# Third layer normalisation moved into the expert loop of a transformer-mixer kernel, near experts' gating and summing fused, output stored by batch

## The chip, the cores and the metric

The kernel runs on one core of a Trainium2 chip. The time is device microseconds of one execution; a measured time is the median of several runs. The core's engines are TensorE (PE, with PEld for its weight loads), VectorE (DVE), ScalarE (ACT), GpSimd (POOL) and SyncE (SP), which here only issues DMA. Everything is float32.

## What is computed

The input x has 8 batches of 512 tokens, 128 features each. Four residual steps follow, each on a layer-normalised x:

```python
x = x + attention(layernorm(x))       # 16 heads, top-k, relative positions: most of the time
x = x + ffn(layernorm(x))             # experts, first call
x = x + mixer(layernorm(x))           # a state-space mixer; step sizes softplus(xn @ W_dt + bias)
x = x + ffn(layernorm(x))             # experts, second call, same weights
```

`ffn` has 8 experts. Each token goes to the expert with the largest logit, if fewer than 512 tokens before it went there; its output is gate * (xn @ W_e + b_e). The kernel computes all eight experts' products for each token and multiplies them by eight gates, of which at most one is not zero, then adds the eight results and the bias product gates @ b.

## The kernel before

**Layout.** The stream `k.X` is [128, 4096] in SBUF: 32 tiles of 128 tokens (partitions) by 128 features. A group is four tiles, 512 tokens, one batch; there are 8 groups. `k.XNT` is the normalised stream, transposed, features on the partitions. Both stay in SBUF for the whole kernel. There are eight PSUM banks of 128 x 512.

**Order of the program.** `attention`, `experts` (first call), `norm`, `mixer`, `norm`, `experts` (second call), `store_stream`. Each part is one or more blocks; a block has one instruction stream per engine, the engines meet only in semaphores, and all engines end a block together. Attention already contains the second normalisation by groups (`group_stats`, `group_rstd`, `group_scale`, `group_turn`, `group_keep`, `group_products`), so the first call of `experts` begins with finished logits in bank 3.

**The helpers by group**, all of which exist before the change and are used in attention: `group_stats` (VectorE, L204: four bn_stats, four bn_aggr, one addition; raises `vareps`), `group_rstd` (GpSimd, L217: a power; raises `rstd`), `group_scale` (VectorE, L223: four tensor_scalar of 128 x 128, (x - mean) * rstd with two scalars from SBUF, L227; raises `scaled`), `group_turn` (TensorE, L232: waits for `scaled`, four transposes into one bank; raises `turned`), `group_keep` (ScalarE, L242: bank to XNT; raises `kept`), `group_products` (TensorE, L248: waits for `kept`, four 128 x 8 products, which the trace shows as eight instructions).

**`norm`** (L1934) normalises all 32 tiles in a block of its own: statistics, powers, scaling, transposes, copies. After it the mixer makes all step sizes in one go (`eight_tensor`, L1223: 32 products of eight columns, 64 instructions) into bank 0, and VectorE copies them (L1233).

**`experts`**, its first block: softmax, place in the expert's queue and the gates `b.gate8` [128, 256], a chain mostly on VectorE. Its second block is the expert loop, written with `two_at_a_time` (two rounds written out, then a hardware loop over pairs, addresses from registers). For each group i:

- SP copies the group's 512 columns of XNT to `xs` and its gates to `gs` by DMA inside SBUF.
- TensorE transposes the gates of the four tiles to bank 4 or 5, then for each tile c makes two products of 512 columns: near (experts 0 to 3) into bank 0 or 2, far (experts 4 to 7) into bank 1 or 3. Each is two instructions in the trace. Behind tile 0 it makes the bias products of the whole group into bank 6 or 7. It waits for `near_scaled` and `far_scaled` of the tile two before, which used the same banks.
- ScalarE copies the turned gates (`gt`), then scales the far bank, four passes of 128 columns each with one gate column (L1401), into `far`.
- VectorE multiplies the near bank with the gates in one pass of 512 columns into `near` (L1426), adds `far` into `sums` (L1418), and adds the bias bank to the stream once a group (L1435).
- GpSimd adds the eight parts of each token: 1024 columns (L1448), 512 (L1451), then into the stream (L1456). It starts when all four tiles of a group are summed (`summed`) and raises `stream_added`.

**`store_stream`** writes all of X to DRAM in one DMA behind the last block.

Of the kernel before, what the change touches and what calls it, by code (L numbers as in the profile page):

```python
# [16 lines left out]
P = 128  # L17
# [1222 lines left out]
def experts(nc, sem, sb, ps, k, r, tag, made=None):  # L1240
# [5 lines left out]
    xs_in = [S(f"xs_in{q}") for q in range(2)]  # L1246
    gs_in = [S(f"gs_in{q}") for q in range(2)]
    g_turned, g_kept, bias_made, bias_added = (S(n) for n in ("g_turned", "g_kept", "bias_made", "bias_added"))

    near_made, y_made, near_scaled, far_scaled = (S(n) for n in ("near_made", "y_made", "near_scaled", "far_scaled"))  # L1250
# [19 lines left out]
    xs = [sb(f"{tag}_xs{q}", [P, 512]) for q in range(2)]  # L1270
    gs = [sb(f"{tag}_gs{q}", [P, 4 * E]) for q in range(2)]
    gt = [sb(f"{tag}_gt{q}", [E, 512]) for q in range(2)]
    near = [sb(f"{tag}_near{q}", [P, 512]) for q in range(2)]
# [67 lines left out]

    with nc.Block() as block:
        @block.sync
        def _(sp):
            def body(i, par, first):
                at, gates_at, free, turned = known(sp, i * 512, i * 4 * E, (i - 1) * 4, i - 1)
                if not first:
                    sp.wait_ge(y_made, free)
                sp.dma_start(xs[par][:, :], k.XNT[:, bass.ds(at, 512)]).then_inc(xs_in[par], 16)  # L1349
                if not first:  # L1350
                    sp.wait_ge(g_turned, turned)
                sp.dma_start(gs[par][:, :], b.gate8[:, bass.ds(gates_at, 4 * E)]).then_inc(gs_in[par], 16)

            two_at_a_time(sp, GROUPS, body)

        @block.tensor
        def _(pe):
            def body(i, par, first, half=0):
                pe.wait_ge(gs_in[par], (half + 1) * 16)
                if not first:  # L1360
                    pe.wait_ge(g_kept, i - 1)
                for c in range(4):
                    last = nc.tensor.transpose(ps[4 + par][0:E, c * P:(c + 1) * P], gs[par][:, c * E:(c + 1) * E],  # L1363
                                               k.ident[:, :])
                last.then_inc(g_turned, 1)
                pe.wait_ge(xs_in[par], (half + 1) * 16)
                for c in range(4):
                    for q in range(2):
                        bank = ps[2 * (c % 2) + q]
                        if not (first and par == 0 and c < 2):  # L1370
# [4 lines left out]
                            .then_inc((near_made, y_made)[q], 1)  # L1375
                    if c == 0:

                        pe.wait_ge(g_kept, i + 1)
                        if not first:
                            pe.wait_ge(bias_added, i - 1)  # L1380
                        for cc in range(4):
                            last = nc.tensor.matmul(ps[6 + par][:, cc * P:(cc + 1) * P],  # L1382
                                                    gt[par][:, cc * P:(cc + 1) * P], r.eb[:, :], start=True, stop=True)
                        last.then_inc(bias_made, 1)

            two_at_a_time(pe, GROUPS, body, with_half=True)

        @block.scalar
        def _(act):
            def body(i, par, first):  # L1390
                act.wait_ge(g_turned, i + 1)
                if not first:
                    act.wait_ge(bias_made, i - 1)
                nc.scalar.activation(gt[par][:, :], ps[4 + par][0:E, :], ACT.Copy).then_inc(g_kept, 1)

                for c in range(4):
                    act.wait_ge(y_made, i * 4 + c + 1)
                    if not (first and par == 0 and c < 2):
                        act.wait_ge(summed, i * 4 + c - 1)
                    for e in range(4):  # L1400
                        last = nc.scalar.activation(far[c % 2][:, e * P:(e + 1) * P],  # L1401
                                                    ps[2 * (c % 2) + 1][:, e * P:(e + 1) * P],
                                                    ACT.Copy, scale=b.gate8[:, bass.ds((i * 4 + c) * E + 4 + e, 1)])
                    last.then_inc(far_scaled, 1)

            two_at_a_time(act, GROUPS, body)

        @block.vector
        def _(dve):
            def body(i, par, first):  # L1410
                def add(c):

                    t = i * 4 + c
                    dve.wait_ge(near_scaled, t + 1)
                    dve.wait_ge(far_scaled, t + 1)
                    if c == 0 and not first:
                        dve.wait_ge(stream_added, i - 1)
                    nc.vector.tensor_tensor(sums[par][:, c, :], near[c % 2][:, :], far[c % 2][:, :],  # L1418
                                            ALU.add).then_inc(summed, 1)

                for c in range(4):
                    t = i * 4 + c
                    dve.wait_ge(near_made, t + 1)
                    if not (first and par == 0 and c < 2):
                        dve.wait_ge(summed, t - 1)
# [4 lines left out]
                    if c > 0:  # L1430
                        add(c - 1)
                    else:
                        X4 = k.X[:, bass.ds(i * 512, 512)]
                        dve.wait_ge(bias_made, i + 1)
                        nc.vector.tensor_tensor(X4, ps[6 + par][:, :], X4, ALU.add).then_inc(bias_added, 1)  # L1435
                add(3)

            two_at_a_time(dve, GROUPS, body)

        @block.gpsimd  # L1440
        def _(pool):

            def body(i, par, first):
                four = sums[par][:, :, :].rearrange("p t (e f) -> p t e f", e=4)
                pool.wait_ge(summed, i * 4 + 4)
                if not early(i):
# [8 lines left out]
                X4 = k.X[:, bass.ds(i * 512, 512)].rearrange("p (t f) -> p t f", t=4)  # L1455
                nc.gpsimd.tensor_tensor(X4, one_sum[:, :, :], X4, ALU.add).then_inc(stream_added, 1)  # L1456

            two_at_a_time(pool, GROUPS, body)
# [6 lines left out]
def mixer(nc, sem, sb, ps, k, r):  # L1465
# [3 lines left out]
    g = eight_sems(sem, "mixer_dt")  # L1469
# [14 lines left out]
    with nc.Block() as block:  # L1484
        @block.tensor
        def _(pe):
            eight_tensor(nc, pe, g, r.wdt[:, :], k.XNT, ps[0])

# [17 lines left out]
        def _(dve):  # L1506
            eight_vector(nc, dve, g, b.raw, ps[0])
            dve.wait_ge(g.stored, 1)
# [450 lines left out]
def store_stream(nc, sem, k, out):  # L1959
    done = sem("stream_stored")  # L1960
    with nc.Block() as block:
        @block.sync
        def _(sp):
            sp.dma_start(out.rearrange("b (t p) d -> p (b t) d", p=P),
                         k.X[:, :].rearrange("p (t d) -> p t d", d=D)).then_inc(done, 16)
# [101 lines left out]
```

## Time and profile before

| | us |
|---|---|
| median of 3 runs | 2992.06 (2991.2 to 2996.38) |
| the profiled execution's own time | 2988.63 |
| its span, first to last instruction | 2986.9 |
| attention and everything before it, until the first logits | 2359.9 |
| first expert loop, first transposes to last sums | 73.1 |
| from there to the mixer's copy of the step sizes | 41.9 |
| second expert loop | 72.3 |
| from the last sums to the end of the span | 14.7 |

How the views are read: a row of the windows view has start and end of a stretch, its length, the busy us and number of instructions of PE, PEld, DVE, ACT and POOL, then PEclk (TensorE's granted clock, 1.00 is full speed), the share of the DMA engines and GB/s. A row of the timeline has start, length, engine, line, operation, the tensors written and read, their sizes, how many instructions of that kind follow each other (x4: the length is that of all four) and in brackets how long the engine was idle before and which instruction released it. Lengths of neighbours on one engine overlap a little, since the next one starts while the last one drains. A row of groups has busy us and mean ns of one.

### The profile page before, as it was taken

The numbers are of one execution on the slowest core, as the hardware profiler recorded it, in microseconds if no ns is written. First come the engines' busy times: TensorE is split into PE (matmuls) and PEld (weight loads), VectorE is DVE, ScalarE is ACT, GpSimd is POOL, SyncE is SP. The second block draws the span as 40 slices with busy tenths as digits, with TensorE's granted clock in tenths as the row PEclk, the third lists the DMA queues.
The fourth block names the chain that finished last, engine by engine and source line by source line (L and its number), as shares of the span: only waits on it lengthen the run. The fifth ranks groups of instructions, "written<-read, shape, count | busy, mean of one in ns | idle before, by whom it ended". The sixth has DMA issues, their size and how long they took to land. (4 is left out here: it accounts for less than half of the span.)

```text
span 2986.9 us, 56920 instructions
## 1 busy us (share of the span) xinstructions
PE 2534.7 (85%) x16480; PEld 1489.4 (50%) x16480; DVE 2680.1 (90%) x6614; ACT 2062.6 (69%) x6275; POOL 2254.1 (75%) x2816
## 2 busy tenths in 40 slices
PE   5788888888888888888888888888888777988857
PEld 3444444444444444444544444444444436777743
DVE  7999999999999999999999999999999374776546
ACT  3788888888888788888887878888887342222214
POOL 4899999998998999999999989999998251222105
PEclk8899999999999999999999999999999786776659
DMA  4444444444444444444444444444443000000001
GB/s 123 121 120 118 121 121 120 121 121 120 120 121 115 120 119 124 121 123 119 122 117 118 123 117 120 122 120 124 119 121 101 12 19 15 8 8 0 1 12 47
DMA packets 373454, 286.18 MB, mean 96 GB/s; under 512 B 30174, under 2 KB 369192, under 8 KB 373160
## 3 DMA queue, kind: packets, MB, share of 16 engines
q1 hardware_dynamic: 372232, 280.62, 33.0%
q8 instruction: 129, 2.11, 0.3%
q10 hardware_dynamic: 928, 2.10, 0.2%
q14 instruction: 165, 1.35, 0.1%
HBM read 139.48 MB, written 136.58 MB: 92 GB/s over the span
## 5 line engine op out<-in xcount | busy, mean ns | idle before, releaser
L1038 DVE MAX8 top<-work 128x8 f32<-128x512 f32 x1536 | 982.8, 684 | 0.0
L1047 DVE MATCH_REPLACE8 work<-top,work 128x512 f32<-128x512 f32 x1024 | 687.4, 682 | 0.0
L1124 POOL TENSOR_TENSOR scores<-scores,cut 128x512 f32<-128x512 f32 x512 | 642.0, 1276 | 0.0
L657 PE MATMUL bank<-probs_t,u 128*64 128x512 f32 x2048 | 476.8, 608 | 10.9 <-ACT u L893 1.4
L1116 POOL TENSOR_SCALAR cut<-scores,minus_max_and_least 128x512 f32<-128x512 f32 x512 | 354.2, 692 | 46.9
L945 ACT ACTIVATE probs_of_tile<-scores,minus_max_and_least 128x512 f32<-128x512 f32 x512 | 376.2, 767 | 14.4 <-POOL scores L1124 14.4
L1137 POOL TENSOR_SCALAR probs_of_tile<-probs_of_tile,inverse 128x512 f32<-128x512 f32 x512 | 349.2, 692 | 26.9 <-DVE inverse L1004 1.4
L1047 DVE MATCH_REPLACE8 work<-top,scores 128x512 f32<-128x512 f32 x512 | 343.6, 682 | 0.0
L1035 DVE MAX8 top<-scores 128x8 f32<-128x512 f32 x512 | 326.7, 683 | 5.2 <-ACT scores L886 4.9
L1120 POOL TENSOR_SCALAR cut<-cut 128x512 f32<-128x512 f32 x512 | 305.6, 613 | 21.5
L864 ACT ACTIVATE band<-band 128x129 f32<-128x129 f32 x512 | 155.2, 304 | 225.1 <-DMA band<-probs_scratch 224.2
L886 ACT ACTIVATE scores<-bank 128x512 f32<-128x512 f32 x512 | 273.3, 584 | 45.1 <-PE bank L706 45.0
L910 ACT ACTIVATE probs_t<-bank 128x512 f32<-128x512 f32 x512 | 282.0, 609 | 11.4 <-PE bank L753 10.3
L753 PE MATMUL bank<-identity,probs_of_tile 128*128 128x128 f32 x2048 | 278.4, 281 | 4.1 <-POOL probs_of_tile L1137 4.1
L657 PEld LDWEIGHTS bank<-probs_t,u 128*64 128x64 f32 x2048 | 137.8, 139 | 267.8 <-issue 228.0
L741 PE MATMUL bank<-identity,band 128*128 128x128 f32 x512 | 109.8, 297 | 185.5 <-ACT band L873 184.1
L657 PE MATMUL bank<-probs_t,v 128*64 128x384 f32 (+1 forms) x2048 | 255.4, 392 | 0.0
L753 PEld LDWEIGHTS bank<-identity,probs_of_tile 128*128 128x128 f32 x2048 | 242.7, 145 | 4.5 <-POOL probs_of_tile L1137 4.5
L657 PEld LDWEIGHTS bank<-probs_t,v 128*64 128x64 f32 x2048 | 124.3, 139 | 173.1 <-ACT probs_t L910 99.0
L1769 POOL TENSOR_TENSOR mixer_a_spread<-rest_after,mixer_a 128x1024 f32<-128x1024 f32 x32 | 66.4, 2075 | 168.8 <-PE bank L1626 137.6
L678 PE MATMUL bank<-keys_left,qt 64*128 64x64 f32 (+3 forms) x1024 | 185.5, 439 | 1.3 <-ACT scores L886 1.3
L923 ACT ACTIVATE rel<-bank 128x254 f32<-128x254 f32 x512 | 174.3, 414 | 1.9 <-PE bank L694 1.9
(274 smaller groups left out, 5005.6 us busy)
## 6 DMA issues: line engine op xcount, KB each, us to landing
probs_scratch<-probs_of_tile SPq DMA_DIRECT2D x256, 256.0 KB, 2.4
band<-probs_scratch SPq DMA_DIRECT2D x256, 256.0 KB, 3.2
rel_scratch<-rel SPq DMA_DIRECT2D x256, 254.0 KB, 3.1
relj<-rel_scratch SPq DMA_DIRECT2D x256, 128.0 KB, 2.3
relj<-rel_scratch SPq DMA_DIRECT2D x512, 64.0 KB, 2.4
experts_xs<-stream_normed_t SPq DMA_DIRECT2D x16, 256.0 KB, 2.3
stream<-in_L_attn_a_x SPq DMA_DIRECT2D x4, 512.0 KB, 7.9
mixer_xs<-stream_normed_t SPq DMA_DIRECT2D x8, 256.0 KB, 2.4
```

The lines of the kernel that those rows point to most:

```text
L657: last = nc.tensor.matmul(U[HEADS[h], lo:hi], lhs, pt[mpar][:, h, jt, lo:hi], start=(jt == 0 and lo == 0), stop=(jt == NT - 1 and step > 0))
L753: last = nc.tensor.transpose(PT[h][:, jt * P:(jt + 1) * P], t.prob[Td][:, h, HALF + jt * P:HALF + (jt + 1) * P], k.ident[:, :])
L886: nc.scalar.activation(sc[Tb][:, h, :], SC[h][:, :], ACT.Copy).then_inc(s.scores_kept, 1)
L910: nc.scalar.activation(pt[dpar][:, h, :, Td * P:(Td + 1) * P], PT[h][:, :].rearrange("p (j i) -> p j i", j=NT), ACT.Copy).then_inc(s.probs ...
L945: nc.scalar.activation(t.prob[Tx][:, h, HALF:HALF + N], sc[Tx][:, h, :], ACT.Exp, bias=neg[q][:, h, 0:1], accum_out=rs[Tx][:, h:h + 1]).th ...
L1035: nc.vector.max(top[q][:, h, 0:8], sc[Tc][:, h, :]).then_inc(s.tops, 1)
L1038: nc.vector.max(top[q][:, h, 8 * rnd:8 * rnd + 8], work[:, h, :]).then_inc(s.next_tops, 1)
L1047: nc.vector.match_replace(out=work[:, h, :], in_to_replace=top[q][:, h, 8 * rnd:8 * rnd + 8], in_values=sc[Tc][:, h, :] if rnd == 0 else w ...
L1116: nc.gpsimd.tensor_scalar(cut[:, h, :], sc[Tc][:, h, :], neg[q][:, h, 1:2], STEEP, ALU.add, ALU.mult).then_inc(s.compared, 1)
L1120: nc.gpsimd.tensor_scalar(cut[:, h, :], cut[:, h, :], 0.0, NEG, ALU.min, ALU.max).then_inc(s.cut, 1)
L1124: nc.gpsimd.tensor_tensor(sc[Tc][:, h, :], sc[Tc][:, h, :], cut[:, h, :], ALU.add).then_inc(s.masked, 1)
L1137: nc.gpsimd.tensor_scalar(row, row, inv[Ty][:, h:h + 1], 1.0, ALU.mult, ALU.mult).then_inc(s.probs, 1)
```

## The change

1. The expert loops are written out, all eight groups, with constant addresses. The copies to `xs` and `gs` go away: TensorE reads XNT and `gate8` directly. Gates use bank 4 alone, bias products bank 6 alone.
2. Near experts: the multiplication into `near` and the addition into `sums` become four scalar_tensor_tensor passes of 128 columns, near bank * gate + far. They wait for `near_made` and `far_scaled`; TensorE waits for `summed` instead of `near_scaled`.
3. The first call of `experts` gets `follow`, the semaphores of a third normalisation by groups, made with the helpers above inside the loop. The step sizes' products go to bank 7. The `norm` block ahead of the mixer and the mixer's own `eight_tensor` go away.
4. The second call gets `out`: SP stores each group when it is finished. `store_stream` goes away.

```diff
+    GT, TURN, BIAS, EIGHT = ps[4:8]
+        if out is not None:
+            @block.sync
+            def _(sp):
+                for i in range(GROUPS):
+                    sp.wait_ge(stream_added, i + 1)
+                    sp.dma_start(out[i, :, :].rearrange("(t p) d -> p t d", p=P),
+                                 k.X[:, i * 512:(i + 1) * 512].rearrange("p (t d) -> p t d", d=D)).then_inc(out_stored, 16)
...
         @block.tensor
+            def late(i):
+                group_turn(nc, pe, follow, i, gw.xn[:, i % 2, :], TURN, k.ident, 1)
+            for i in range(GROUPS):
...
+                    last = nc.tensor.transpose(GT[0:E, c * P:(c + 1) * P], b.gate8[:, at:at + E], k.ident[:, :])
                 last.then_inc(g_turned, 1)
+                if follow and i >= 2:
+                    late(i - 2)
                 for c in range(4):
                     for q in range(2):
-                            pe.wait_ge((near_scaled, far_scaled)[q], i * 4 + c - 1)
-                        nc.tensor.matmul(bank[:, :], xs[par][:, c * P:(c + 1) * P],
+                        if t >= 2:
+                            pe.wait_ge((summed, far_scaled)[q], t - 1)
+                        nc.tensor.matmul(ps[2 * (c % 2) + q][:, :], k.XNT[:, t * P:(t + 1) * P],
...
+                    if c == 2 and follow and i >= 2:
+                        group_products(nc, pe, follow, i - 2, follow.W, k.XNT, EIGHT)
+            if follow:
+                for i in range(GROUPS - 2, GROUPS):
+                    late(i)
+                    group_products(nc, pe, follow, i, follow.W, k.XNT, EIGHT)
...
         @block.scalar
+                    if c == 0 and follow and i >= 2:
+                        group_keep(nc, act, follow, i - 2, TURN, k.XNT)
...
         @block.vector
+            def stats(i):
+                dve.wait_ge(stream_added, i + 1)
+                group_stats(nc, dve, follow, gw, k.X, i)
+            def scale(i):
+                if i >= 2:
+                    dve.wait_ge(follow.turned, i - 1)
+                group_scale(nc, dve, follow, gw, k.X, i, gw.xn[:, i % 2, :])
+            for i in range(GROUPS):
                 for c in range(4):
                     t = i * 4 + c
                     dve.wait_ge(near_made, t + 1)
-                    nc.vector.tensor_tensor(near[c % 2][:, :].rearrange("p (e f) -> p e f", e=4),
-                                            ps[2 * (c % 2)][:, :].rearrange("p (e f) -> p e f", e=4),
-                                            b.gate8[:, bass.ds(t * E, 4)].unsqueeze(2).to_broadcast([P, 4, P]),
-                                            ALU.mult).then_inc(near_scaled, 1)
+                    dve.wait_ge(far_scaled, t + 1)
+                    for e in range(4):
+                        cols = slice(e * P, (e + 1) * P)
+                        last = nc.vector.scalar_tensor_tensor(
+                            out=sums[par][:, c, cols], in0=ps[2 * (c % 2)][:, cols],
+                            scalar=b.gate8[:, t * E + e:t * E + e + 1], in1=far[c % 2][:, cols],
+                            op0=ALU.mult, op1=ALU.add)
+                    last.then_inc(summed, 1)
...
+                    if c == 2 and follow and i:
+                        stats(i - 1)
+                if follow and i:
+                    scale(i - 1)
+            if follow:
+                stats(GROUPS - 1)
+                scale(GROUPS - 1)
...
         @block.gpsimd
                 nc.gpsimd.tensor_tensor(X4, one_sum[:, :, :], X4, ALU.add).then_inc(stream_added, 1)
+                if follow:
+                    group_rstd(nc, pool, follow, gw, i)
...
 in mixer:
-            eight_tensor(nc, pe, g, r.wdt[:, :], k.XNT, ps[0])
-            eight_vector(nc, dve, g, b.raw, ps[0])
+            dve.wait_ge(made.products, GROUPS)
+            nc.vector.tensor_copy(b.raw[:, :], ps[7][:, 0:n8]).then_inc(raw_kept, 1)
...
 in program:
+            experts(nc, sem, allocate(ctx), ps, k, r, "experts1", norm2, norm3, gw)
+            mixer(nc, sem, allocate(ctx), ps, k, r, norm3)
         norm(nc, norms, ps, k, w)
+            experts(nc, sem, allocate(ctx), ps, k, r, "experts2", out=out)
```

## Rows read from the trace of the kernel before

**Rows 1.** Windows by stage (columns are explained above): first loop, behind it, the mixer.
```profile
2372.59:2445.67 73.08, 71.00 (x224) 34.10 (x224) 53.21 (x72) 40.17 (x136) 35.28 (x21) 0.97 0.08 27
...
2445.67:2487.57 41.90, 22.12 (x96) 19.44 (x96) 17.98 (x81) 4.78 (x8) 10.83 (x5) 0.54 0.00 0
...
2487.57:2850.89 363.32, 308.12 (x1574) 251.30 (x1574) 228.47 (x641) 98.74 (x191) 74.78 (x40) 0.69 0.02 6
```

**Rows 2.** Timeline of the second expert loop, TensorE and ScalarE.
```profile
2910.31 1.88 PE L1373 MATMUL bank<-rest_we,experts_xs 128*128 128x512 f32 x4
...
2913.21 5.42 PE L1373 MATMUL bank<-rest_we,experts_xs 128*128 128x512 f32 x12
...
2915.23 1.14 ACT L1401 ACTIVATE experts_far<-bank,experts_gate 128x128 f32<-128x128 f32 x4 [1.86 <-PE bank L1373]
...
2916.95 1.14 ACT L1401 ACTIVATE experts_far<-bank,experts_gate 128x128 f32<-128x128 f32 x4 [0.57 <-PE bank L1373]
...
2961.83 1.88 PE L1373 MATMUL bank<-rest_we,experts_xs 128*128 128x512 f32 x4
```

**Rows 3.** Chain that ended last: start us, us, what; handover from ScalarE to VectorE.
```profile
2919.43 0.39 ACT experts_far L1401
...
2919.91 0.70 DVE experts_sums L1418
```

**Rows 4.** Groups of VectorE by line and shape, whole span.
```profile
L1426 DVE TENSOR_TENSOR experts_near<-bank,experts_gate 128x512 f32<-128x512 f32 x64 | 44.2, 690 | 24.7 <-PE bank L1373 19.2 <-DVE experts_sums L1418 5.1
...
L1805 DVE SCALAR_TENSOR_TENSOR mixer_sum_x<-mixer_conv_x,rest_cwx,mixer_sum_x 128x512 f32<-128x512 f32 x24 | 17.7, 737 | 0.0
...
L1877 DVE TENSOR_TENSOR stream<-bank,stream 128x128 f32<-128x128 f32 x16 | 4.6, 286 | 15.5 <-PE bank L1676 15.5
```

**Rows 5.** Timeline at the end of set_up: scaling alone, then beside GpSimd.
```profile
34.46 1.11 DVE L227 TENSOR_SCALAR probs_t<-stream,group_mean_var,group_rstd 128x128 f32<-128x128 f32 x4
...
38.05 2.49 POOL L1068 TENSOR_TENSOR stream<-stream,attention_out_bias 128x512 f32<-128x512 f32 x2
...
38.11 2.52 DVE L227 TENSOR_SCALAR probs_t<-stream,group_mean_var,group_rstd 128x128 f32<-128x128 f32 x2
```

**Rows 6.** Timeline of the last 15 us.
```profile
2971.54 0.69 DVE L1418 TENSOR_TENSOR experts_sums<-experts_near,experts_far 128x512 f32<-128x512 f32 x1 [0.40 <-ACT experts_far L1401]
...
2972.31 2.34 POOL L1448 TENSOR_TENSOR experts_two_sums<-experts_sums 128x1024 f32<-128x1024 f32 x1 [3.22 <-DVE experts_sums L1418]
...
2976.25 1.26 POOL L1456 TENSOR_TENSOR stream<-experts_one_sum,stream 128x512 f32 x1 [0.26 <-POOL experts_one_sum L1451]
...
2977.80 0.39 SPq L1964 DMA_DIRECT2D out_stream<-stream  x1
```

**Rows 7.** Timeline at the start of the first expert loop.
```profile
2370.03 0.55 SPq L1349 DMA_DIRECT2D experts_xs<-stream_normed_t  x1
...
2372.59 1.02 PE L1363 MATMUL bank<-identity,experts_gs 128*8 128x128 f32 x4 [7.51 <-DMA experts_gs<-experts_gate]
...
2373.40 3.62 PE L1373 MATMUL bank<-rest_we,experts_xs 128*128 128x512 f32 x4
```

**Rows 8.** DMA issues: KB each, median us to landing.
```profile
experts_xs<-stream_normed_t SPq DMA_DIRECT2D x16, 256.0 KB, 2.3
```

**Rows 9.** Timeline of the last group normalised in attention.
```profile
2351.46 0.87 DVE L207 BATCH_NORM_STATS2 group_stats<-stream 128x6 f32<-128x128 f32 x4 [20.36 <-POOL stream L1097]
...
2355.26 1.11 PE L238 MATMUL bank<-identity,keys_right 128*128 128x128 f32 x4 [3.29 <-DVE keys_right L227]
...
2356.16 3.42 PE L252 MATMUL bank<-rest_wg,stream_normed_t 128*128 128x8 f32 x16
...
2356.47 0.60 ACT L245 ACTIVATE stream_normed_t<-bank 128x512 f32<-128x512 f32 x1 [4.66 <-PE bank L238]
```

**Rows 10.** Timeline of the mixer: scaling of its output beside GpSimd.
```profile
2626.83 2.96 DVE L1921 TENSOR_SCALAR mixer_yn<-mixer_yz,mixer_n_mean,mixer_n_rstd 128x256 f32<-128x256 f32 x4
...
2627.05 1.95 POOL L1769 TENSOR_TENSOR mixer_a_spread<-rest_after,mixer_a 128x1024 f32<-128x1024 f32 x1 [1.28 <-PE bank L1626]
```

More of the change, by code:

```diff
@@ L1233, in eight_vector, with experts @@
     nc.vector.tensor_copy(OUT[:, :], bank[:, 0:TILES * 8]).then_inc(s.stored, 1)
-def experts(nc, sem, sb, ps, k, r, tag, made=None):
+def experts(nc, sem, sb, ps, k, r, tag, made=None, follow=None, gw=None, out=None):
     def S(n):
@@ L1340, in _ @@
             link(nc.vector.tensor_tensor(v3(b.gate8), v3(b.keep), over(b.prob), ALU.mult))
+    GT, TURN, BIAS, EIGHT = ps[4:8]
     with nc.Block() as block:
[L1343 to L1354, printed above, removed]
+        if out is not None:
[5 more added lines that the diff above has]
+                                 k.X[:, i * 512:(i + 1) * 512].rearrange("p (t d) -> p t d", d=D)).then_inc(out_stored, 16)
+                sp.wait_ge(out_stored, 16 * GROUPS)
@@ L1391, in body @@
                 act.wait_ge(g_turned, i + 1)
-                if not first:
+                if i >= 2:
                     act.wait_ge(bias_made, i - 1)
-                nc.scalar.activation(gt[par][:, :], ps[4 + par][0:E, :], ACT.Copy).then_inc(g_kept, 1)
+                nc.scalar.activation(gt[par][:, :], GT[0:E, :], ACT.Copy).then_inc(g_kept, 1)
                 for c in range(4):
-                    act.wait_ge(y_made, i * 4 + c + 1)
-                    if not (first and par == 0 and c < 2):
-                        act.wait_ge(summed, i * 4 + c - 1)
+                    t = i * 4 + c
+                    act.wait_ge(far_made, t + 1)
+                    if t >= 2:
+                        act.wait_ge(summed, t - 1)
@@ L1408, in _ @@
+            if follow:
+                for i in range(GROUPS - 2, GROUPS):
+                    group_keep(nc, act, follow, i, TURN, k.XNT)
         @block.vector
         def _(dve):
[L1410 to L1419, printed above, removed]
+            def stats(i):
+                dve.wait_ge(stream_added, i + 1)
+                group_stats(nc, dve, follow, gw, k.X, i)
@@ L1421, in body @@
+            def scale(i):
+                if i >= 2:
+                    dve.wait_ge(follow.turned, i - 1)
+                group_scale(nc, dve, follow, gw, k.X, i, gw.xn[:, i % 2, :])
+            for i in range(GROUPS):
+                par = i % 2
                 for c in range(4):
@@ L1430, in body @@
[L1430 to L1433, printed above, removed]
-                        dve.wait_ge(bias_made, i + 1)
-                        nc.vector.tensor_tensor(X4, ps[6 + par][:, :], X4, ALU.add).then_inc(bias_added, 1)
-                add(3)
-            two_at_a_time(dve, GROUPS, body)
+                    dve.wait_ge(far_scaled, t + 1)
+                    if c == 0 and i >= 2:
+                        dve.wait_ge(stream_added, i - 1)
@@ L1440, in _ @@
+                    if c == 2 and follow and i:
[5 more added lines that the diff above has]
+                scale(GROUPS - 1)
         @block.gpsimd
         def _(pool):
-            def body(i, par, first):
+            for i in range(GROUPS):
+                par = i % 2
                 four = sums[par][:, :, :].rearrange("p t (e f) -> p t e f", e=4)
                 pool.wait_ge(summed, i * 4 + 4)
-                if not early(i):
+                if i:
@@ L1956, in norm @@
     s.before += 1
[L1959 to L1965, printed above, removed]
-            sp.wait_ge(done, 16)
 def program(nc, a, out):
```

62 lines of the change are left out of this document (25 added, 37 removed).

## Prediction

> **What bounds the kernel now.** I read the row of slices on the page first, then the windows view by stage, then the order of time inside one expert loop. Attention, the first 2360 us, and the mixer's 363 us are not touched [rows 1]. What is touched are the two expert loops, 73 us each, the 41.9 us between the end of the first and the mixer's first copy, in which TensorE works 22 us at a granted clock of 0.54, and the last 14.7 us, from the last sums at 2972.23 [rows 6] to the end of the span.
>
> Inside an expert loop TensorE sets the pace: one group of four tiles (512 tokens) follows the other in (2961.83 - 2910.31) / 6 = 8.59 us, at full clock [rows 2]. Measured from the first product of the group ("near 0"): near 1 starts 2.90 later, and from there each tile takes 1.72, as the spacing of ScalarE's far passes shows [rows 2]. So near 1 to near 3 is 3.44 and near 3 to the next near 0 is the rest, 2.25. VectorE (53 us of 73), ScalarE (40) and GpSimd (35) have room [rows 1]. This works because a near bank is given back by VectorE's own pass, which waits for nothing but the product.
>
> **The change in both loops: the bank's way back.** The near pass (multiply) and the sum become four 128-column scalar_tensor_tensor passes, which need the far tile too. A near bank then comes free only after both products, ScalarE and VectorE: near start to ScalarE's start 2.02 [rows 2], four far passes 1.14 [rows 2], handover 0.09 (2919.82 to 2919.91 [rows 3]), four passes, the same handover. The trace has no such pass. Per instruction: two inputs and 128 columns take 0.286, and a pointer scalar adds 0.737 - 0.690 = 0.047 at 512 columns [rows 4]; four without overlap would be 1.33. The floor is one 512-column pass, 0.69. I take 1.11, the time of four 128-column passes with pointer scalars [rows 5]. Near start to "group's tile summed" is then 2.02 + 1.14 + 0.09 + 1.11 = 4.36, and to the bank's reuse 4.45. TensorE wants near 3 only 3.44 after near 1: a stall of 1.00 per group. Elsewhere the bias products or the gate transposes fill the distance. In the second loop that is 8 x 1.00, and 0.30 more behind the last near 3 (4.36 against 2972.23 - 2961.83 - 2.90 - 3.44 = 4.06): **+8.3**.
>
> **The two starts.** The copies of normed tokens and gates go away. The first transposes began 2.56 after the first DMA issue (2370.03 to 2372.59 [rows 7]) and can now start at that point: **-2.6** twice.
>
> **The stores.** Before, GpSimd ends at 2977.51, 5.28 after the sums; the 2 MB store is issued 0.29 later, and the span ends 9.10 after that issue [rows 6]. After, seven batches go out during the loop; the last one is 256 KB. A copy of that size inside the chip lands after 2.3 [rows 8]; this one goes to DRAM in 512-byte rows, I put 3.2 to the end of the span (ends: 2.3 and 9.1). GpSimd needs 5.1, the 5.28 without most of its 0.26 idle for an address that is now written out [rows 6]. 5.1 + 0.1 + 3.2 = 8.4 instead of 14.7: **-6.3**. Second call together: 8.3 - 2.6 - 6.3 = **-0.6**.
>
> **The third normalisation inside the first loop.** What it takes away: between the last sums (2445.67) and the mixer's copy (2487.57) lie 41.9 [rows 1]. After, the last group needs GpSimd's three sums, 5.2, and then the chain that the trace shows for the last group of attention: statistics to the end of ScalarE's keep, 2356.47 + 0.60 - 2351.46 = 5.6 [rows 9]; eight products of eight columns at the low clock, half of 3.42, 1.7 [rows 9]; block end 0.35. Together 12.9: **-29.0**. Transposes and products of the other groups lie inside the loop; eight products fit the new stall before near 3 (16 take 3.42 at low clock, so 0.9 at full clock against 1.00). ScalarE's keep, 0.6, lies in its idle time, and the statistics fall between tile 2 and tile 3, where VectorE waits for ScalarE. These cost nothing while TensorE stalls there anyway; without that cover they would cost 0.9 a group.
>
> What it adds is a wait. TensorE's `late(i - 2)` stands right behind the gate transposes of group i. It needs `scaled`, and VectorE scales group i - 2 only at the end of its round i - 1, behind the passes of tile 3. TensorE stands there 2.25 after near 3, VectorE finishes tile 3 at 4.36 (call this T). Behind the waiting transposes are queued all products of group i, and ScalarE and VectorE wait for those. So in groups 2 to 7 the scaling lies on the path that sets the end, and its length counts.
>
> Alone it takes 1.11 [rows 5]. But at T GpSimd starts its own three passes of the group, 2.34, 1.26 and 1.26 with handovers, until T + 5.1 [rows 6]. The trace shows the very same scaling instruction beside GpSimd's tensor_tensor: four take 1.11 alone, but two take 2.52 beside two GpSimd passes of together 2.49, one each, in step with them [rows 5]; in the mixer four of the same form, 256 columns wide, take 2.96, and 1.95 of that is a GpSimd pass in the middle [rows 10]. So I expect one scaling before the first GpSimd pass and one behind each of the three: end at T + 5.2. The Trainium skill, "SBUF — State Buffer", section "Who interferes with whom", states that a tensor_scalar in a two-port mode and a GpSimd instruction lock each other out for the whole instruction; the trace agrees. By that rule and by the rows the sum is the same; without either it would be the first rival's.
>
> TensorE is then idle for 4.36 + 5.2 - 2.25 = 7.3 in each group. At the start of the loop, behind the gates' chain on VectorE, the first four product instructions took 3.62 instead of 1.88 [rows 2, 7], and the loop's granted clock of 0.97 over 73.1 us [rows 1] amounts to 4.4 us at the lower of the two levels (1.2 GHz instead of 2.4). In attention's last group 3.29 of idling was enough: the four transposes behind it took 1.11 [rows 9]. So I let each of these groups start at the lower level: 1.74 more from near 0 to near 1. One group: near 0 to near 3 2.90 + 4.45 + 1.74 = 9.09; to T 4.36; scaling 5.2; start and slow transposes until near 0 0.95: **19.6**, instead of 8.59. Sum: group 0 +1.0; group 1, still warm, 17.85 - 8.59 = 9.3; five groups x 11.0 = 55.0; the last, near 0 to T, 9.09 + 4.36 - 10.40 = 3.0: **+68.3**. First call: 68.3 - 29.0 - 2.6 = **+36.7**.
>
> **At nothing:** loops written out instead of registers (TensorE's pace shows no loop cost), single banks for gates and bias (given back a whole group earlier), the mixer's copy from another bank, SP's queue, which loses 32 issues that nothing waits for after the start.
>
> **Sum.** 36.7 - 0.6 = +36.1. Span 2986.9 to 3023.0; the profiled execution's own time 2988.6 to 3024.7; the median of the runs lies 3.4 above that: 2992.1 to **3028**.
>
> **Rivals.**
> - *No lock-out.* The four scalings take 1.11 beside GpSimd's sums. Groups 2 to 7 then take 2.90 + 4.45 + 4.36 + 1.11 + 0.5 = 13.3, if TensorE's clock holds over 3.2 of idling: 1.0 + 6 x 4.7 + 1.3 = 30.5, and in all 30.5 - 29.0 - 2.6 - 0.6 = -1.7: **2990**. Against it speaks what VectorE did beside GpSimd [rows 5, 10]; for it nothing but that this pair of instructions was not seen. The point that decides is a group of 13.6 us: below, the kernel is not slower. With passes at their floor (0.42 less at 24 places) it would be 2980. If the clock falls all the same, 2.1 a group come back: 3003.
> - *Two scalings slip into each gap.* The last ends behind the second GpSimd pass, T + 3.9: 6 x 1.3 less, **3020**. In setup it was one per gap [rows 5].
> - *The new passes are locked out too.* The near passes, from PSUM with one SBUF input, were not: 690 ns in the mean of all 64 [rows 4], but these read a pointer scalar as well. Tile 0's four passes would then step along with GpSimd's: ready at T + 1.1, done at T + 5.4 instead of 2.3, about 3 us in each of the 8 group changes without `late`: +24, **3052**.
> - *The clock stays low for the whole group*, as in the mixer (0.69 at 85% busy [rows 1]). A tile costs 3.5, near 1 to near 3 with products 8.7 instead of 4.45, T 1.7 later: +6.0 in six groups, **3064**; for half of them 3046.
>
> **Chances.** Forecast 0.55 (its own range 3012 to 3038: passes 0.69 to 1.33 move it by -10 and +5, the clock's 1.74 by up to -10 if it recovers at once); two per gap 0.10; no lock-out 0.15, of which 0.05 below and 0.06 within 0.2%; new passes locked out 0.10; low clock 0.10. 0.2% is 6 us, about what a measurement of this kernel tells from no change. The range 3010 to 3056 leaves out "no lock-out" and the worse half of the last. Faster 0.05, same 0.06, slower 0.89.
>
> **What the profile after would show.** In the first loop: near 0 to near 0 of groups 2 to 7 some 19 to 20 us, TensorE idle 7 us behind the gate transposes with VectorE's scaling as releaser, scaling instructions of 1.3 to 2.4 us each, a clock near 0.7 or 0.8. In the second loop: groups of 9.6, a 1.0 us stall before near 3, clock 1.0. Between the last sums and the mixer's copy 13 us. A last store landing in under 3.5. I am wrong if the scaling runs in 1.1 beside GpSimd, or if TensorE's waits in the first loop are released by something else.

## The result, and the profile after

The changed kernel takes 3040.12 us (median of 4 runs, 3028.62 to 3049.8), the kernel before 2991.63 (4 runs on the same chip, 2988.97 to 2996.38): ratio 1.0173, 95% interval 1.0141 to 1.0206. The profiled execution took 3049.8 us, with a span of 3048.1. That execution is the slowest of the four, 9.7 above their median, which matters when its stages are added up.

The windows of the kernel after, by stage: first loop, from there to the mixer's first copy, mixer, second loop. The columns are those of [rows 1].

```profile
2372.66:2530.49 157.83, 110.06 (x296) 55.47 (x296) 81.84 (x224) 43.08 (x142) 41.31 (x28) 0.72 0.00 0
2530.49:2543.52 13.03, 5.98 (x24) 4.99 (x24) 7.71 (x18) 1.19 (x2) 5.91 (x4) 0.61 0.00 0
2543.52:2948.46 404.94, 335.56 (x1670) 273.44 (x1670) 247.79 (x720) 103.52 (x199) 80.05 (x42) 0.66 0.02 6
2958.63:3040.30 81.67, 73.30 (x224) 33.56 (x224) 40.83 (x136) 40.17 (x136) 34.19 (x21) 0.97 0.08 23
```

Against [rows 1] the first loop is 157.83 instead of 73.08 (+84.8; forecast +68.3), at a granted clock of 0.72 instead of 0.97. The stretch behind it is 13.03 instead of 41.90 (-28.9; forecast -29.0). The second loop, from its first transposes to its last sums, is +9.4 (forecast +8.3).

The timeline of the kernel after, where two groups of the first loop meet:

```profile
2391.84 1.98 PE L1369 MATMUL bank<-rest_we,stream_normed_t 128*128 128x512 f32 x4 [0.74 <-DVE experts_sums L1433]
2392.38 1.13 DVE L1433 SCALAR_TENSOR_TENSOR experts_sums<-bank,experts_gate,experts_far 128x128 f32<-128x128 f32 x4 [0.59 <-ACT experts_far L1402]
...
2396.15 5.30 DVE L227 TENSOR_SCALAR group_xn<-stream,group_mean_var,group_rstd 128x128 f32<-128x128 f32 x4
2396.31 2.37 POOL L1458 TENSOR_TENSOR experts_two_sums<-experts_sums 128x1024 f32<-128x1024 f32 x1 [0.32 <-DVE experts_sums L1433]
2398.76 1.26 POOL L1461 TENSOR_TENSOR experts_one_sum<-experts_two_sums 128x512 f32<-128x512 f32 x1
2400.10 1.26 POOL L1466 TENSOR_TENSOR stream<-experts_one_sum,stream 128x512 f32<-128x512 f32 x1
2401.50 1.11 PE L238 MATMUL bank<-identity,group_xn 128*128 128x128 f32 x4 [7.24 <-DVE group_xn L227]
```

Read it from the bottom: TensorE idles 7.24 us in front of the transposes of the group two back, released by VectorE's scaling. The scaling's four instructions take 5.30 from first to last, and end with GpSimd's third pass. That is the place and the length that the prediction gave (7.3 and 5.2). The chain of products, ScalarE, fused pass costs 0.74 of idling in front of near 3 (first row).

What was not foreseen is what TensorE does next. The same view, TensorE alone, two later groups:

```profile
2402.41 3.62 PE L1369 MATMUL bank<-rest_we,stream_normed_t 128*128 128x512 f32 x4
2405.96 2.07 PE L1377 MATMUL bank<-rest_eb,experts_gt 8*128 8x128 f32 x8
2407.96 6.64 PE L1369 MATMUL bank<-rest_we,stream_normed_t 128*128 128x512 f32 x8
...
2446.95 1.12 PE L238 MATMUL bank<-identity,group_xn 128*128 128x128 f32 x4 [7.24 <-DVE group_xn L227]
2447.85 3.62 PE L1369 MATMUL bank<-rest_we,stream_normed_t 128*128 128x512 f32 x4
2451.40 1.16 PE L1377 MATMUL bank<-rest_eb,experts_gt 8*128 8x128 f32 x8
2452.49 3.70 PE L1369 MATMUL bank<-rest_we,stream_normed_t 128*128 128x512 f32 x8
```

Both groups come out of a 7.24 us wait at the lower clock level: four products 3.62 instead of 1.88. In the group of 2447.85 the clock is back for the bias products (1.16), and the next group follows 19.65 later (2447.85 to 2467.50), which is the forecast 19.6. In the group of 2402.41 the bias products still take 2.07 and the next eight products (tiles 1 and 2) 6.64 instead of 3.70; the next group follows after 23.39. Five of the six groups with a long wait go this second way, with eight products between 5.12 and 6.72 long, and the five distances between the six are 23.39, 22.05, 19.65, 23.49 and 23.69: 14.3 more than five times 19.6. The last group, 15.81 to its last sums, adds 2.4 to its 13.45.

The end of the kernel after, in its timeline:

```profile
3040.38 2.34 POOL L1458 TENSOR_TENSOR experts_two_sums<-experts_sums 128x1024 f32<-128x1024 f32 x1 [4.55 <-DVE experts_sums L1433]
...
3044.13 1.26 POOL L1466 TENSOR_TENSOR stream<-experts_one_sum,stream 128x512 f32<-128x512 f32 x1
```

From the last sums at 3040.30 to the end of the span are 7.8 us, against 14.7 before [rows 6]: -6.9 (forecast -6.3). The starts of the two loops are 2.5 shorter each (forecast 2.6). What is left of the 61.2 us between the two spans, 2.6 in attention and 5.2 in the mixer and the norm behind it, lies in code that the change doesn't touch.

### The profile page after: what moved, and what is told of

It reads as the page before. It is cut to its first block and busy times, and to the rows that moved or that the text cites. A ratio compares the mean times of both kernels' runs of the same rounds, so it can differ in the third digit from the quotient of the medians.

```text
span 3048.1 us, 56228 instructions
## 1 busy us (share of the span) xinstructions
PE 2569.5 (84%) x16480; PEld 1501.1 (49%) x16480; DVE 2689.9 (88%) x6767; ACT 2063.9 (68%) x6275; POOL 2253.4 (74%) x2822
## 5 line engine op out<-in xcount | busy, mean ns | idle before, releaser
L1038 DVE MAX8 top<-work 128x8 f32<-128x512 f32 x1536 | 1014.6, 726 | 0.0
L1047 DVE MATCH_REPLACE8 work<-top,work 128x512 f32<-128x512 f32 x1024 | 708.5, 723 | 0.0
L1047 DVE MATCH_REPLACE8 work<-top,scores 128x512 f32<-128x512 f32 x512 | 353.9, 722 | 0.0
L1035 DVE MAX8 top<-scores 128x8 f32<-128x512 f32 x512 | 337.2, 723 | 7.8 <-ACT scores L886 7.2
L1433 DVE SCALAR_TENSOR_TENSOR experts_sums<-bank,experts_gate,experts_far 128x128 f32<-128x128 f32 x256 | 72.1, 345 | 117.4 <-ACT experts_far L1402 76.0
```

The source lines that it names most:

```text
L1035: nc.vector.max(top[q][:, h, 0:8], sc[Tc][:, h, :]).then_inc(s.tops, 1)
L1038: nc.vector.max(top[q][:, h, 8 * rnd:8 * rnd + 8], work[:, h, :]).then_inc(s.next_tops, 1)
L1047: nc.vector.match_replace(out=work[:, h, :], in_to_replace=top[q][:, h, 8 * rnd:8 * rnd + 8], in_values=sc[Tc][:, h, :] if rnd == 0 else w ...
```

## The experiments

Theory: VectorE's scaling beside GpSimd's sums, waited for by TensorE in front of each group, makes the first loop long; the clock's late recovery adds to it; the fused near passes cost 1 us a group. Rivals: the scaling's place alone is at fault, GpSimd alone is, or the clock carries nearly all. Experiments ran on other chips than the first comparison, so each is given by its ratio to the kernel before on its own chip; by ratio, 0.01 is 29.9 us. The kernel after stands at 1.0173, which is 52 us (the medians alone differ by 48.5). The expectations in microseconds are on the scale of the first chip, where the kernel before took 2991.63; on that scale the first four runs below are 3001, 3007, 3021 and 2970.

**The scaling moved away from TensorE.** Transposes of group i - 2 behind tile 3 of group i, products and keep a group later; nothing else.

```diff
-                if follow and i >= 2:
-                    late(i - 2)
...
+                if follow and i >= 2:
+                    late(i - 2)
             if follow:
+                group_products(nc, pe, follow, GROUPS - 3, follow.W, k.XNT, EIGHT)
```

> The changed kernel with late(i - 2) moved from ahead of group i's first product to behind its last one, keep and step sizes' products one group later. Theory A (the place of the wait and the lock-out): TensorE no longer waits for the scaling, but VectorE's four scalings still step along with GpSimd's sums until T + 5.3, and tile 0 of the next group is queued behind them on VectorE. Near 2 then starts 8.0 us after near 0 instead of 4.6, a group takes 13.5 instead of 19.6 to 23.7, the first loop about 109 us instead of 158: 2998 (2991 to 3010). Theory B (only the place of the wait counts, scaling is hidden once TensorE doesn't wait for it): groups of 10.2, loop 85: 2975. Theory C (the loss comes from the fused passes and the written-out loops, not from this wait): 3030 to 3040.

Measured: 2989.22 us (10 runs), ratio 1.0031 (1.0013 to 1.0049). The first loop is 110.71. Its timeline shows where the wait went:

```profile
2395.59 5.31 DVE L227 TENSOR_SCALAR group_xn<-stream,group_mean_var,group_rstd 128x128 f32<-128x128 f32 x4
...
2400.82 1.11 DVE L1434 SCALAR_TENSOR_TENSOR experts_sums<-bank,experts_gate,experts_far 128x128 f32<-128x128 f32 x4
2401.99 5.40 PE L1367 MATMUL bank<-rest_we,stream_normed_t 128*128 128x512 f32 x8 [3.57 <-DVE experts_sums L1434]
```

The scaling is as slow as before. TensorE no longer waits for it, but the pass of tile 0 is queued behind it on VectorE, so the near bank comes back late and TensorE idles 3.57 in front of near 2. Some 42 us of the 52 are gone; what stays is the same scaling, felt in another place, as theory A had it.

**GpSimd held back.** The sums of group i start behind the scaling; TensorE's order is the changed kernel's.

```diff
                     pool.wait_ge(stream_added, i)
+                    if follow:
+                        pool.wait_ge(follow.scaled, i)
```

> The changed kernel, but GpSimd starts the sums of group i only when VectorE has scaled group i - 1, so that the scalings run alone; late stays where it is. Theory A: four scalings take 1.1 instead of 5.3, a group takes 13.4 if TensorE's clock holds over 3.2 us of idling, 15 to 19 if it falls: 2993 to 3015, and GpSimd's sums, 1.1 later, cost nothing. Rival (the four scalings are slow by themselves, not because of GpSimd): they still take 5.3, and GpSimd starts later: 3040 or more.

Measured: 2990.89 us (10 runs), ratio 1.005 (1.0028 to 1.0071). Its timeline, at two places:

```profile
2402.22 1.10 DVE L227 TENSOR_SCALAR group_xn<-stream,group_mean_var,group_rstd 128x128 f32<-128x128 f32 x4
2403.38 0.66 PE L238 MATMUL bank<-identity,group_xn 128*128 128x128 f32 x4 [3.04 <-DVE group_xn L227]
2403.49 2.34 POOL L1460 TENSOR_TENSOR experts_two_sums<-experts_sums 128x1024 f32<-128x1024 f32 x1 [1.43 <-DVE group_xn L227]
...
2429.99 1.12 PE L238 MATMUL bank<-identity,group_xn 128*128 128x128 f32 x4 [3.04 <-DVE group_xn L227]
...
2434.45 2.07 PE L1377 MATMUL bank<-rest_eb,experts_gt 8*128 8x128 f32 x8
```

With GpSimd waiting 1.43 us more, the same four scalings take 1.10 instead of 5.30, and TensorE's wait falls from 7.24 to 3.04. This shows the cause of the long scaling. Some 37 us of the 52 are gone. The rule that the prediction drew on, in the Trainium skill, "SBUF — State Buffer", section "Who interferes with whom", that a tensor_scalar in a two-port mode and a GpSimd instruction block each other for the whole instruction, agrees; which mode the scaling ran in, no run shows. The second place shows that after the very same wait of 3.04 the transposes are sometimes slow and the clock late: in two of the six groups.

**The clock held.** Eight 512-column products of constants (16 instructions in the trace), ahead of TensorE's wait, into the bank that the transposes overwrite; they start when ScalarE has copied the group before out of it.

```diff
+                    if i >= 3:
+                        pe.wait_ge(follow.kept, i - 2)
+                    for _ in range(8):
+                        nc.tensor.matmul(TURN[:, :], k.ident[:, :], r.we[:, 0:512], start=True, stop=True)
                     late(i - 2)
```

> The changed kernel with eight products of 512 columns into the bank that late(i - 2) is about to overwrite, ahead of its wait: 6.9 us of work in 7.2 us of idling, results overwritten. Theory A with the clock as a part of the loss: each group starts at full clock, takes 17.5 instead of 19.65 or 23.5, and the runs lie closer together: 3014 (3008 to 3020). If the clock is no part: 3040, or more where the added work is in the way.

Measured: 3009.94 us (4 runs), ratio 1.0099 (1.0061 to 1.0137); the first loop is 132.34 at a granted clock of 0.95. Its timeline:

```profile
2406.37 7.03 PE L1366 MATMUL bank<-rest_we,identity 128*128 128x512 f32 x16
2413.78 0.66 PE L238 MATMUL bank<-identity,group_xn 128*128 128x128 f32 x4 [0.38 <-DVE group_xn L227]
2414.27 1.88 PE L1373 MATMUL bank<-rest_we,stream_normed_t 128*128 128x512 f32 x4
2416.08 1.15 PE L1381 MATMUL bank<-rest_eb,experts_gt 8*128 8x128 f32 x8
```

The wait for the scaling ends where it did, but every product behind it runs at full clock, and groups follow each other in 17.50, as expected. The whole loop is 157.83 - 132.34 = 25.5 us shorter, but that difference is too small for the clock's price in the groups with a wait: this execution happened to begin its loop slowly (14.77 from near 0 of group 0 to near 0 of group 1, against 11.04), ahead of any added product. From near 0 of group 1 to the last sums it is 116.77 against 145.98, so the clock was worth 29.2 us there. The prediction had 13.1 for it: six times 1.74 on the products and 0.45 on the transposes. By the ratios it is 22 us, with an uncertainty of 15, and the run's 3021 lies 1 above its expected range of 3008 to 3020. The rival that the clock carries nearly all the loss is refuted: with the clock held the kernel still stands at 1.0099.

**Both moves.** Scaling's transposes later and GpSimd behind the scaling.

```diff
-                if follow and i >= 2:
-                    late(i - 2)
...
+                if follow and i >= 2:
+                    late(i - 2)
...
+                    if follow:
+                        pool.wait_ge(follow.scaled, i)
```

> Both moves of the first two: late behind tile 3, and GpSimd's sums behind the scaling. Theory A: neither TensorE nor VectorE waits, groups of 10.2 us, first loop 84: 2975 (2970 to 2982). Theory B expects the same as for the first of these kernels, 2975 for both. Theory C: 3030 to 3040.

Measured: 2954.85 us (10 runs), ratio 0.9928 (0.9909 to 0.9948): faster than the kernel before. Its timeline:

```profile
2403.63 1.88 PE L1367 MATMUL bank<-rest_we,stream_normed_t 128*128 128x512 f32 x4
...
2405.24 1.11 DVE L227 TENSOR_SCALAR group_xn<-stream,group_mean_var,group_rstd 128x128 f32<-128x128 f32 x4
...
2410.97 1.99 PE L1367 MATMUL bank<-rest_we,stream_normed_t 128*128 128x512 f32 x4
...
2413.67 1.88 PE L1367 MATMUL bank<-rest_we,stream_normed_t 128*128 128x512 f32 x4
```

Groups follow each other in 10.04 (2403.63 to 2413.67), and the first loop is 83.27 long. One move alone took off 42 us, the other 37; together they take off 73, since TensorE no longer waits for anything in front of a group and the clock stays up. The norm is still not free there: without it a group takes 9.60 with the same passes, as the next runs show.

**The change taken apart.** Three kernels: the near passes separate again (the norm inside); the norm back between loop and mixer (the passes fused); both undone, so that the loops written out and the single stores are left. The pass and the norm as undone:

```diff
-                        last = nc.vector.scalar_tensor_tensor(
-                            out=sums[par][:, c, cols], in0=ps[2 * (c % 2)][:, cols],
...
+                    nc.vector.tensor_tensor(near[c % 2][:, :].rearrange("p (e f) -> p e f", e=4),
+                                            ps[2 * (c % 2)][:, :].rearrange("p (e f) -> p e f", e=4),
...
+                    nc.vector.tensor_tensor(sums[par][:, c, :], near[c % 2][:, :], far[c % 2][:, :],
+                                            ALU.add).then_inc(summed, 1)
```

```diff
-            experts(nc, sem, allocate(ctx), ps, k, r, "experts1", norm2, norm3, gw)
+            experts(nc, sem, allocate(ctx), ps, k, r, "experts1", norm2)
+        norm(nc, norms, ps, k, w)
```

> Only the near experts' passes are undone: one multiplication from the bank and a sum of its own, as in the kernel before; the third norm stays inside the first loop and the batches stay stored singly. Theory A (the four fused passes hold the near bank 1.12 us instead of 0.69, which costs the second loop its measured +9.4 us and is part of the first loop's +84.8): groups of the second loop back at 8.6 us, so 9.4 off there, and 0 to 10 off the first loop, where the stall behind the scaling covers most of it; in all 9 to 19 below the changed kernel, 29 to 39 above the kernel before, ratio about 1.010 to 1.013. Rival B (the fused passes cost nothing, the second loop's +9.4 is the single stores or the placement of the banks): second loop stays at 81.7, ratio stays at 1.017. Rival C (the separate sums, which read SBUF twice as the sums on GpSimd's side do, are now kept off by GpSimd in the first loop too, beside the scaling): the first loop gets longer than 157.8 and the ratio is 1.017 or more.

> Only the third norm is taken out of the first loop again, a block between the loop and the mixer as in the kernel before, with the mixer's step sizes made there; the loop written out, the fused passes and the single stores stay. Theory A (the norm inside costs 84.8 less the fused passes' share and gives back 28.9): both loops at 9.6 us a group, 81.7 each, the stretch between loop and mixer at 41.9 again, the ends of both loops 2.5 and 6.9 shorter: 8 groups x 1.0 x 2 = +17 to +19, less 2.5 + 2.5 + 6.9 = 12: 5 to 8 above the kernel before, ratio 1.002 to 1.003. Rival B (the loop written out or the fused passes themselves bring the long groups of the first loop): first loop well over 82, ratio 1.01 or more.

> The third norm taken out of the loop and the near passes undone: what is left of the change is the loop written out instead of run by the engines' loop registers, and the last group's batches stored singly. Theory A (the two are worth what the profile of after shows at the loops' edges: 2.5 us at each start and 6.9 at the end, and the groups cost what they cost before, 8.6 to 8.7 us): 10 to 12 below the kernel before, ratio 0.996 to 0.997. Rival B (these edges were gained only because something else moved, such as the norm's idle time before the mixer): within 3 us of the kernel before, ratio 0.999 to 1.001.

| ratio to the kernel before (95% interval) | near passes fused | separate | fused costs |
|---|---|---|---|
| norm inside the loop | 1.0173 (1.0141 to 1.0206) | 1.0098 (1.0065 to 1.0132) | 0.0075 = 22 us |
| norm behind it | 1.0026 (1.0008 to 1.0044) | 0.9953 (0.9928 to 0.9979) | 0.0073 = 22 us |
| norm inside costs | 0.0147 = 44 us | 0.0145 = 43 us | |

The rest, 0.9953, is 14 us gained by the single stores and the loops written out, which no run separates; 10 to 12 were expected. Of the other two, the one with the norm behind the loop and fused passes came out as expected (1.002 to 1.003), and the one with the norm inside and separate passes just below its 1.010 to 1.013. Within the intervals the two losses add. The windows of the first loop with the norm behind it, first with fused passes and then with separate ones:

```profile
2365.34:2449.14 83.80, 75.44 (x224) 34.76 (x224) 40.80 (x136) 40.17 (x136) 34.18 (x21) 0.94 0.00 1
```
```profile
2370.31:2442.70 72.39, 70.41 (x224) 34.05 (x224) 53.37 (x72) 40.27 (x136) 36.53 (x21) 0.98 0.00 1
```

VectorE has less to do with fused passes (40.80 against 53.37 us) and the loop is longer: groups of 9.60 instead of 8.59. Over 16 groups that is 16 us; the clock came back later at this loop's start, which is 3 of the 11.4. The ratios' 22 carry an uncertainty of 9 or more, so they don't contradict 16.

With the norm inside and separate passes all five distances between the groups with a wait are 20.5, and the clock is back for the bias products in each of the six; so the 8.4 us between the two loops (157.83 against 149.42) go with the late recovery. The waits differ as well: 8.30 in front of the transposes,

```profile
2413.03 5.30 DVE L227 TENSOR_SCALAR group_xn<-stream,group_mean_var,group_rstd 128x128 f32<-128x128 f32 x4 [0.91 <-POOL group_rstd L220]
...
2418.38 1.12 PE L238 MATMUL bank<-identity,group_xn 128*128 128x128 f32 x4 [8.30 <-DVE group_xn L227]
2419.29 3.52 PE L1371 MATMUL bank<-rest_we,stream_normed_t 128*128 128x512 f32 x4
2422.75 1.15 PE L1379 MATMUL bank<-rest_eb,experts_gt 8*128 8x128 f32 x8
```

because in this kernel the statistics stand behind tile 3's near pass and GpSimd's rstd comes 0.91 late. The pair of kernels is therefore not a clean measure of the fused passes in that loop; the pair with the norm behind it is.

**The parts that paid, together.** Both moves and separate passes in both loops; then fused passes in the first loop only, beside a repetition of the former.

> The best of the parts together: the scaling and its transposes one group later and behind the fourth tile, GpSimd's sums behind the scaling (both as in the run that was 21 us below the kernel before), and in addition the near passes undone. Theory A (the fused passes are the rest of the loss in both loops: groups there 10.0 and 9.6 us against 8.6 before): second loop 9.4 off, first loop 5 to 9 off, so 14 to 18 below that run, 35 to 40 below the kernel before, ratio 0.987 to 0.988. Rival B (the separate sums on VectorE and GpSimd's sums keep each other off while the scaling waits between them, so the first loop gives the gain back): 9 below that run at most, ratio 0.990 or more.

> The scaling one group later and GpSimd's sums behind it, as in both runs that beat the kernel before; the near passes fused in the first loop only, and separate in the second. Theory A (each loop takes the form that its profile showed to be shorter): groups of 10.0 us in the first loop (the run with fused passes, where the run with separate ones had 10.5 to 11.4) and of 8.6 us in the second (where fused ones took 9.6): 4 to 6 us below the kernel with separate passes in both loops, ratio to the kernel before 0.986 to 0.989. Rival B (the difference of the first loop's groups was that one execution's): the same time as that kernel within 2 us, ratio 0.989 to 0.991.

> The kernel with the scaling later, GpSimd's sums behind it and separate near passes in both loops once more, beside the one with fused passes in the first loop on the same chip, so that the two can be compared: theory A 0.989 to 0.991 of the kernel before, as it was (0.9897), and 4 to 6 us above the other; rival B level with it.

Measured: separate in both 2954.78 us (4 runs), ratio 0.9897 (0.9864 to 0.9931); fused in the first loop only 2957.43 (6 runs), 0.9902 (0.9877 to 0.9927); separate in both again 2966.03 (8 runs, 2943.05 to 2975.06), 0.992 (0.9888 to 0.9952). The timeline of the first of these, where the sums meet GpSimd:

```profile
2409.87 2.35 POOL L1471 TENSOR_TENSOR experts_two_sums<-experts_sums 128x1024 f32<-128x1024 f32 x1 [1.32 <-DVE group_xn L227]
...
2410.35 1.98 PE L1369 MATMUL bank<-rest_we,stream_normed_t 128*128 128x512 f32 x4 [1.18 <-DVE experts_near L1442]
...
2411.41 1.36 DVE L1434 TENSOR_TENSOR experts_sums<-experts_near,experts_far 128x512 f32<-128x512 f32 x1
```

Here the separate sum takes 1.36 instead of 0.69 beside GpSimd's passes, and the groups are 10.5 to 11.4 long, against 10.03 with fused passes. So the 14 to 18 us that theory A gave the separate passes over the kernel with both moves did not come; by ratio it is 9 us in one measurement and 2 in the other, as rival B had it. In the profiles of the first of these and of the kernel with both moves, the second loop gives 11 us (72.57 against 83.77), and the first takes 4 back (87.49 against 83.27); a part of both is the clock at the loops' starts. Fused and separate passes in the first loop cannot be told apart by the times: their intervals lie over each other, and the 4 to 6 us of the last theory A is neither shown nor refuted. Nor is either kernel shown to beat the one with both moves alone. All three kernels beat the kernel before, by 0.7 to 1.0%.

## Why the prediction was right, step by step

- **Direction and size.** 3028 was forecast, 3040.12 measured, inside the range, but 2 us beyond the 3012 to 3038 that the prediction gave its own mechanism. The changes' sum was +36.1; the profiled spans differ by 61.2, the medians by 48.5.
- **Scaling locked out, one instruction per gap of GpSimd's passes: right.** T + 5.2 was forecast, and the four took 5.30 from T; the run with GpSimd held back shows that this is the cause. In the trace the first of the four took 0.34 and the longest 2.37, as long as GpSimd's first pass, and the last ended with the third. That refutes the rivals "no lock-out" and "two slip into each gap".
- **The wait in front of each group: right,** 7.24 against 7.3, and group 1, which still starts warm, is 17.90 long (2384.51 to 2402.41) against 17.85.
- **The clock: right in kind, too small.** The step "1.74 more from near 0 to near 1" is the term that was mis-sized: I took the one recovery that [rows 7] show, within the first four products. Five of six groups recovered later, the slowest near the end of the eight products behind the bias. The clock's price was 29.2 us, by the run that held it, where 13.1 stood in the sum; that is 16.1 of the 16.5 that the first loop went beyond its forecast. The trace is that of the slowest of four executions, so how much of this the other three paid stays open. Nor was one case of idling a measure for all: after 3.29 the clock had fallen in [rows 9], after 3.04 in two groups of six. The rival "the clock stays low for the whole group" is half true: in the slowest groups to near the end of tile 2, not of the group.
- **The fused passes: right.** Four took 1.12 to 1.13 (forecast 1.11), near 1 to near 3 was 4.44 (2387.40 to 2391.84; forecast 4.45), of which the profile shows 0.74 as the wait, and a group 9.60 (forecast 9.6). The rival that GpSimd locks them out is refuted: a pass at 2387.67 took 1.13 in the middle of GpSimd's 2.35 at 2386.72. The Trainium skill, "SBUF — State Buffer", section "Who interferes with whom", says that a VectorE instruction with at most one SBUF input outside the two-port modes does not contend with GpSimd, and that one with two contends with a GpSimd instruction that reads SBUF; the fused pass's 1.13 and the separate sum's 1.36 agree.
- **Behind the loop, starts and stores: right,** -28.9 (forecast -29.0), -2.5 twice (-2.6), -6.9 (-6.3). The eight stores of 256 KB landed after 2.3 in the median, and the span ends 2.7 after the last was issued (3.2 in the sum).
- **At nothing: not contradicted.** The loops written out and the single stores together gave 14 us, with an interval of 6 to 22; the edges that the profile shows make 12 of that.

Open: why the clock recovers after four product instructions in one group and only after seven to eleven in the others (an estimate from how much longer than 3.70 the eight products took, at 0.45 for each slow one), with waits of 7.23 to 7.46 us before it and the same products behind. A longer wait is not the reason: with separate passes TensorE waited 8.30, and all six groups recovered after the first four. No run separated more.

## What to carry to other kernels

Work moved into a loop that runs at TensorE's pace is cheap (here 0.4 us a group of 9.60) only if TensorE never waits for its result in program order and no other engine locks out the instruction that makes it; each move alone left the kernel slower than before, both together turned 1.7% slower into 0.7% faster. Fusing two passes saves the engine's time but joins two dependencies: where a bank is given back by the pass, ask what the fused one waits for. And a stall on TensorE can cost more than its length: here 7.24 us of waiting brought 2 to 6 us of slow products behind it.

## What the hardware showed unexpectedly

- After one and the same wait TensorE's clock came back at different points: after the first four products, 3.6 us, in a group of 19.65, and after about the eleventh in one of 23.39, by the estimate above. There the granted clock was 0.50 from 2397.0 to 2413.5, although TensorE worked with hardly a pause from 2401.50 on. After waits of 3.04 us it had fallen in some groups and not in others (transposes 1.12 and 0.66).
- Untouched code differs between the profiled executions by as much as many of the effects at issue: from the mixer's first copy to the second loop's first transposes the profiled executions took 391.97 (with both moves) to 415.11 us (the changed kernel), at granted clocks of 0.69 and 0.66. Differences between stages have to be read at the stage itself, and small ones between kernels from many runs.
